# Mixer stage of a four-part network on one core: PE issues a row's scan after the step's other products instead of among them

## The reference, cut to what matters

```python
zxbcdt = xf @ W_in                                  # z (192), xBC (224), dt (12)
xBC = silu(conv3x3(xBC) + b_conv)                   # x_inner (12 heads x 16), B_state (16), C_state (16)
dt = softplus(dt + dt_bias)
y = ssd_minimal_discrete(x_inner * dt, A * dt, B_state, C_state, ...)   # scan over the tokens
y = y + x_inner * D_param
y = layernorm(y) * gamma + beta
y = y * silu(z)
out = x + y @ W_out
```

## Time and profile before

| | |
|---|---|
| median of 3 runs | 2060.57 us (2054.01 to 2062.62) |
| the profiled execution | 2070.34 us, its span 2068.5 us |
| granted PE clock over the span | 0.896 of full speed |
| busy, share of the span | PE 87%, PEld 68%, DVE 77%, ACT 53%, POOL 60% |
| the row loop of the second mixer | its first scan starts at 798.85 us, its last ends near 1656.6 us |

### The profile page before, as it was taken

How to read it: one execution, slowest core, us unless ns; L and a number is a source line. 1 busy time by engine, 2 the same in 40 slices (tenths; PEclk the granted TensorE clock), 3 DMA queues, 4 the chain that set the end, 5 groups by cost and what they waited for, 6 DMA issues and landing times. The chain is left out here.

```text
span 2068.5 us, 63524 instructions
## 1 busy us (share of the span) xinstructions
PE 1791.5 (87%) x24986; PEld 1403.6 (68%) x24986; DVE 1588.6 (77%) x5061; ACT 1103.0 (53%) x2139; POOL 1238.0 (60%) x1313
## 2 busy tenths in 40 slices
PE   4884763888999949999998999999999959999996
PEld 3772642656777747777777777777777646777775
DVE  6885665966777866888989898988887669777774
ACT  2441411656777746555555554555543226777774
POOL 3337244675578744445476665667664547777776
PEclk9765755998999979999999999999998559999998
DMA  9310002455655662000000000000000025665553
GB/s 145 99 77 32 16 20 94 141 164 178 202 184 176 190 142 37 3 4 3 3 12 10 11 10 11 10 12 11 11 11 9 11 93 166 191 191 192 183 190 122
DMA packets 95404, 174.18 MB, mean 84 GB/s; under 512 B 53256, under 2 KB 66550, under 8 KB 95108
## 3 DMA queue, kind: packets, MB, share of 16 engines
q10 hardware_dynamic: 21312, 102.00, 15.2%
q1 hardware_dynamic: 56516, 41.86, 8.7%
q0 software_dynamic: 17280, 26.26, 3.7%
HBM read 134.71 MB, written 36.72 MB: 83 GB/s over the span
## 5 line engine op out<-in xcount | busy, mean ns | idle before, releaser
L1197 PE MATMUL ps<-rounded 97*128 97x512 f32 (+4 forms) x952 | 392.6, 412 | 19.7 <-DMA rounded<-weights_by_expert 8.0
L1198 PE MATMUL ps<-rounded 97*128 97x512 f32 (+4 forms) x952 | 373.0, 392 | 0.0
L1199 PE MATMUL ps<-rounded 97*128 97x512 f32 (+4 forms) x952 | 372.1, 391 | 0.0
L960 ACT ACTIVATE rounded<-ps 128x512 fp32r<-128x512 f32 (+1 forms) x444 | 259.8, 585 | 209.1 <-PE ps L1199 117.3
L2142 DVE TENSOR_TENSOR rounded<-arena,rounded 128x512 fp32r<-128x512 f32 (+1 forms) x321 | 248.7, 777 | 134.1 <-ACT arena L961 106.3
L1288 PE MATMUL ps<-rounded 128*128 128x464 f32 (+2 forms) x1428 | 320.7, 361 | 0.7 <-ACT rounded L980 0.6
L1288 PEld LDWEIGHTS ps<-rounded 128*128 128x128 f32 x1428 | 240.3, 200 | 51.3 <-issue 5.9
L961 ACT ACTIVATE arena<-ps 128x512 f32<-128x512 f32 (+1 forms) x444 | 260.3, 586 | 0.0
L779 POOL TENSOR_TENSOR w<-arena,consts 128x384 f32<-128x384 f32 x128 | 107.2, 838 | 243.2 <-issue 231.0
L1197 PEld LDWEIGHTS ps<-rounded 97*128 97x128 f32 (+2 forms) x952 | 169.5, 178 | 76.9 <-issue 15.0
L711 POOL TENSOR_TENSOR rounded<-arena,rounded 128x512 fp32r<-128x512 f32 (+1 forms) x123 | 154.3, 1254 | 100.8 <-ACT arena L961 94.8
(11 more groups left out here) (365 smaller groups left out, 3868.6 us busy)
## 6 DMA issues: line engine op xcount, KB each, us to landing
rounded<-weights_by_expert ACTq DMA_DIRECT2D x148, 673.0 KB
arena<-rows SPq DMA_DIRECT2D x68, 208.0 KB
residual<-in_x SPq DMA_DIRECT2D x16, 384.0 KB, 7.1
weights_by_expert<-rounded SPq DMA_DIRECT2D x8, 672.0 KB, 3.8
residual<-after_ffn SPq DMA_DIRECT2D x12, 384.0 KB, 6.6
w<-in_w SPq DMA_DIRECT2D x4, 576.0 KB
rows<-arena SPq DMA_DIRECT2D x11, 208.0 KB
after_ffn<-arena POOLq DMA_INDIRECT x142
```

The lines of the kernel that those rows point to most:

```text
L960: act.activation(hidr[:, 0, c, 0:width(t)], bank(UPS[step % len(UPS)])[:, 0:width(t)], ACT.Gelu)
L1197: pe.matmul(dst, left[0], right[0], start=start, stop=False)
L1198: pe.matmul(dst, left[1], right[0], start=False, stop=False)
L1199: return pe.matmul(dst, left[0], right[1], start=False, stop=stop)
```

## The change

In PE's `step`, the call of `scan` moves from between the two halves of z to the end of the step, straight before `pairs`. Nothing else changes, neither on PE nor on another engine: the same instructions with the same waits, in another order on PE.

```diff
                 if (q := quad(g, r, 4)) is not None:
                     z_columns(g, q, 0)
-                if (i := row(g, r, 7)) is not None:
-                    scan(g, i)
                 if (q := quad(g, r, 5)) is not None:
                     z_columns(g, q, 1)
                 if (k := tile_quad(r, -T_AHEAD)) is not None:
                     to_columns(g, k)
                 if (c := quad(g, r, 15)) is not None:
                     project(g, c)
                 if (c := quad(g, r, U_LAG)) is not None:
                     u_columns(g, c, 0)
                 if (c := quad(g, r, U_LAG + 1)) is not None:
                     u_columns(g, c, 1)
+                if (i := row(g, r, 7)) is not None:
+                    scan(g, i)
                 if (i := row(g, r, 5)) is not None:
                     pairs(g, i)
```

## The result

The changed kernel takes **2106.49 us** (median of 3 runs, 2102.02 to 2108.39), against 2060.57 before: a ratio of 1.0233, 95% interval 1.0188 to 1.0277. In a second session it came to 1.0269 (1.0208 to 1.0329). It is slower, in the range and a little above the forecast of 2090.

A forecast was written before the change was run, and what follows sets the result against it. It took PE to bound quads without routing and the DVE those with routing. Units +15.9, clock +15.6 and front quads -1.7 gave +30 us on the median 2060.57: 2090 us, range 2050 to 2112.

The forecast's parts named there:

- The order of T step and gate: T step: gate, transpositions and scan precede the gather, 2.80 us; routing quads +1.40 us (first), +1.86 (second, third).
- Seams and quads without routing: PE switches to and from 32-column products once per step: 0.21 us saved a step, 0.84 a quad, less the T-step wait.
- T wait: In quads without routing, PE waits 0.41 us at the T step: the DVE needs 5.12 us, PE 4.71.
- such a quad gains 0.43 us: Each quad without routing saves 0.84 us in switches and loses 0.41 waiting, ahead of the units and between them alike.
- The P step in routing quads: Scan behind the projection: +0.71 us in first quads, -0.28 in second and third; the projection wait goes, -0.74.
- The clock: PE's half clock after idling delays the gather: 1.3 us per second and third routing quad, +15.6 in all, bounds 0 and 3.2.
- third rival: Clock also falls in first routing quads and stays at half up to twice as long: 2103 to 2132 us; chance 0.10.
- six units: Six units in the loop, each with three routing quads and one without: 6 x (1.4 + 0.84 + 0.84 - 0.43) = +15.9 us.
- The sum: Whole kernel: +15.9 us from units, +15.6 from the clock, -1.7 from four front quads: +30, 2090 us.
- PE's time counts: Rival: every quad gets shorter by its 0.84 us of switches, 2034 us, or 2052 if only quads without routing gain; chance 0.14.
- A wash: Rival: the T-step wait comes but the DVE gets it back, the clock falls no oftener: 2062 to 2071 us; chance 0.20.
- Slower by more: Rival: 18 routing quads lose 1.6 to 3.2 us each to half clock, in place of 15.6 in all; chance 0.10.

The follow-up runs named there:

- e1: The changed kernel, but the T step keeps its scan ahead of the transpositions: 2046.27 us, ratio 1.0007 to the kernel before.
- e7: e4 plus unread products: four ahead of transpositions in second and third routing quads' T steps, five ahead of the first's S-step scan: 2047.41 us, ratio 1.0001.
- e11: e4 with the rows that POOL writes in the T step issued one step later, in the P step: 2103.57 us, ratio 1.0307.
- e4: The changed kernel with the DVE's second gate product moved from the head of its T step to the end of its S step: 2066.39 us, ratio 1.0111.
- e8: The kernel before, with five unread products ahead of the scan in T steps of second and third routing quads: 2062.73 us, ratio 1.0107.
- e3: The changed kernel with nine unread products ahead of the transpositions in T steps of second and third routing quads: 2080.35 us, ratio 1.0182.
- e6: The changed kernel with the scan late in Z and S steps alone, in its old place in P and T: 2039.09 us, ratio 0.9973.
- e10: The kernel before with the scan late in Z and S, and scan and pairs ahead of the transpositions in T: 2038.5 us, ratio 0.9977.
- e2: The changed kernel with the scan late in T steps alone, in its old place in P, Z and S: 2128.7 us, ratio 1.0435.

## Why the prediction was right, and where its terms were off

**The order of T step and gate.** Right, and in size. The S to T distance in a first quad at full clock is +1.44, predicted +1.40; in a second one +1.82 after the filler's own 0.56, predicted +1.86. In front quads, at full clock in the changed kernel itself, the gather comes 2.76 us after the gate's start, predicted 2.80. e1 and e7 show the cause from two sides: put the scan back in front, or bring the gate forward and keep the clock up for longer, and 32 or 35 of the 55.9 us of the five units are gone, and with the shorter last rows the whole loss.

**Seams and quads without routing.** Right ahead of the units: -0.51, -0.68 and -0.11 us in the three quads that took 25.41 us before, a mean of -0.43, as predicted; with this spread the agreement to the hundredth is luck. T wait 0.25, predicted 0.41; the way out of the scan 0.14 shorter, predicted 0.12. **Wrong between the units**: there the step "such a quad gains 0.43 us" failed, +1.18 in the mean: +2.24, +1.34 and +2.29 in three of the five, nothing in the other two. It is the T to P distance, +1.78, and +1.88 at full clock. Timeline of PE and POOL, a P step in a quad of this kind, in the changed kernel:

```profile
1291.86 0.80 PE L1288 MATMUL ps<-rounded 128*128 128x240 f32 x3
...
1292.45 1.06 POOL L807 DMA_INDIRECT rows<-residual,w  x1 [0.16 <-issue]
...
1293.23 0.49 PE L1288 MATMUL ps<-rounded 128*128 128x224 f32 x3 [0.57 <-issue]
...
1297.54 1.06 POOL L807 DMA_INDIRECT rows<-residual,w  x1 [0.17 <-issue]
...
1298.08 0.25 PE L1356 MATMUL ps<-arena 32*32 32x16 f32 x5 [0.20 <-issue]
...
1298.85 0.63 PE L1356 MATMUL ps<-arena 32*32 32x16 f32 x51 [0.52 <-issue]
```

PE pauses for 0.57 + 0.20 + 0.52 us beside POOL's rows, in convolution and scan, both ahead of the gather: 1.29 of the 2.67 by which T to P grew in this quad. Front quads have no such rows yet, and there T to P still grows by 0.63, 0.62, 1.07 and nothing; the two together are not the whole 2.67. In the two quads between units that lose nothing, POOL's row of the P step starts 0.7 us after that step's gather, in the other three ahead of it. I took a quad ahead of the units as the model of one between them, and POOL as an engine that costs nothing. No run took the rows away, but e11, which puts all three into the P step, loses 24.8 us over these five quads where e4 loses 2.4.

**The P step in routing quads.** Right: +0.71 and -0.28 predicted, +0.54, -0.28 and +0.25 at full clock (first, second, third), and the wait for the projection gone, -0.59 to -0.91 for a predicted -0.74. With the clock as it falls, it is +1.58, +0.97 and +1.51.

**The clock.** The mechanism was right for the new order, its size too small; that the slow stretch was covered in the old one no run shows (e8). Against the predicted steps a second quad loses 3.30 - 1.86 = 1.44 in the T step and 0.97 + 0.28 = 1.25 in the P step, 2.7 us; a third one 1.26 + 1.79 = 3.0, for the 1.3 that I took and the 3.2 that was my bound. First quads, for which I took nothing, lose 0.39 + 0.87 = 1.3: in five of them PE was at half clock for 13.7 us, for none before. That is the first half of the third rival. What failed is the single row as price: it was one stretch of some 3.3 us, and the changed kernel has stretches of 10.24. Per us of added half clock the loss is small: from e3 to the changed kernel 26 us in the five units (29.9, the filler's own time in it, to 55.9) for 106 us more of half clock (6.8 to 112.7).

**The last unit.** The step "six units" failed in the other direction. I gave it +5.25 like the others; its last 21 rows, from gather 105 on, are 11.2 us shorter. Windows of the longest stretch of half clock that reaches into these rows, of the kernel before and of the changed one:

```profile
1609.90:1698.70 88.80, 65.29 (x1079) 46.35 (x1080) 61.22 (x248) 19.56 (x39) 44.70 (x53) 0.50 0.16 57
```
```profile
1657.00:1684.30 27.30, 27.30 (x532) 19.46 (x534) 20.33 (x68) 6.81 (x14) 19.63 (x23) 0.50 0.04 13
```

The two are not of the same place: the first goes on past the loop's last gather (1660.7), the second ends ahead of it (1695.5). Within the 21 rows PE is at 0.50 for 65.6 us before and 44.4 after. They gain 11 to 15 us in the changed kernel, e1, e3 and e4, whose P scan is late, with 27 to 44 us at half clock there. In e6 and e10, with it early, it is 68 and 60 us, and the gain is -0.8 and 1.1. But e2, also with an early P scan, has 44.4 us and gains only 0.9, so the clock is not all of it; what sets the time there stays open.

**The sum.** Five units 55.9 for 26.3 predicted, the front -1.3 for -1.7, the last rows -11.2 for +5: +43 in the loop for +30. The total came as close as it did because two errors of 30 and 16 us have opposite signs; the direction did not depend on them.

**The rivals.** "PE's time counts" fell where I had put its point: the T wait is there, 0.25 us, in the very quads that PE fills. "A wash" fell: half clock came oftener, and nothing was given back in routing quads. "Slower by more" was half true: the clock fell in first quads too, and stretches were up to three times as long, yet the last rows gave 11 us back.

## What to carry to other kernels

Before a step on one engine is moved to save a little time there, write down what it now stands behind, and when the engine that waits for its result would have produced what releases that: a wait of another engine, moved in front of work that this same engine needs, is paid twice. Price an idle stretch of PE by what runs right after it, since the clock was low there (0.50 for 10.24 us behind 4.39 us of idle time), and see who waits for that work. And take each kind of stretch as its own model: the quads ahead of the units and those between them differ in one engine's side work, and that changed the sign.

## What the runs showed of the hardware that I had not expected

PE pauses beside POOL's indirect DMAs, some 0.65 us at a time from one record to the next, in strings of small matmuls and in the convolution, with "issue" as the only cause in the profile. Of the pauses within the scan (distances of over 0.25 us from one record's start to the next at L1356) 15 of 15 overlap such a row before, 48 of 48 in e2, 62 of 65 in e11 (41.2 us in sum there, 6.9 before), and they move when the rows are moved. Why PE pauses there is open.

The granted clock stays at 0.50 through 27.3 us in which PE is busy for all of them (window 1657.00 to 1684.30, above), so PE was busy again here for long without full clock. And filling an idle PE can pay: nine products that nobody reads, ahead of the transpositions, made the loop 22 us shorter in the new order. Five of them ahead of the scan in the old order made it 13 us longer.
